# Causal masks written to PSUM by sixteen 32x32 matrix products instead of four 128x128 ones

## Chip, cores and metric

One core of one Trainium2 chip runs the whole program. The time is that of one execution on the device, in microseconds (us). The kernel before takes 2322.14 us (median of 3 executions, 2321.32 to 2324.43).

## The reference

The input is a batch of 32 sequences of 128 tokens with 512 features, and a context of the same shape. Two layers follow, each with an attention part and a feed-forward part. Cut to what matters here:

```python
# x, ctx: (32, 128, 512)
x = x + wkv(w, u, layernorm(x), ctx)            # recurrence over the tokens, per feature

# 16 heads of 32: causal softmax attention
scores = einsum('bhtd,bhsd->bhts', Qf, Kf) * scale
scores = where(tril(ones(T, T)), scores, finfo.min)     # mask
x = x + (softmax(scores) @ V) @ Wp

# mLSTM over q = layernorm(x), k = v = ctx
log_D = where(tril(ones(s, s)), fg_mat, -inf) + ig      # mask
D = exp(log_D - max(log_D)); C = (q @ k) / sqrt(dh) * D
x = x + headnorm((C / normalizer) @ v)

# 32 experts, the best 8 for each token
x = x + moe(layernorm(x), gate_w, w_gate, w_up, w_down)
```

Both masks set every element above (or, transposed, below) the diagonal of a 128 by 128 square to a very low value.

## The kernel before

The program has two blocks. The first does everything up to the router, one sequence of the batch after the other; the second does the experts. The change touches the first block alone.

**The layer loop.** Each engine has its own instruction stream with a function `step(j, ...)`, and the streams meet in semaphores. A pass j of the loop works on four sequences at once: the recurrence of sequence j (flag `ahead`), the softmax attention of j - 1 (`attn`), the mLSTM of j - 2 (`mlstm`), the router of j - 3 (`route`) and the places of the tokens in the experts' lists (`pairs`). Passes 4 to 31 are a hardware loop in which all flags are set, 28 passes; passes 0 to 3 and 32 to 35 are written out with some of the flags off. The order of the calls in `step` is the order of the work on that engine. Nothing else plans it.

**TensorE's pass** (lines 1168 to 1255): turn kn, q product, turn ctx, turn qn (it waits for VectorE's qn), `scores()`, gates, v product, `max_turn()`, `scores_turned()`, `minus_max()`, spread of the gates (L1106) and of the sums (L1102), places (L1165, L1166), turn of yy (it waits for VectorE's yy, L1384), then waits for the places to be taken (L1204) and for ScalarE's copies of the spread gates Lt and Rt (L1207), `log_d()`, qk, row sums, turn of zn, weighted v, centring, head sums, router, heads back (L1145), turn of xn, projection, k product. A "turn" is four 128x128 transposes into one bank of PSUM (L990).

**The masks.** Scores of the 16 heads lie in four banks of PSUM: bank r holds the heads 4c + r, at columns c * 128 for c = 0 to 3. The heads of a bank have their 32 features on partitions 32r to 32r + 31, so the products of the four banks use four different row tiles of the array (32 rows by 128 columns each). Before the products are added, `masks(bank, mask)` writes the mask to each of the four banks: a product of the 128x128 identity (`identb`, bf16) with the mask, which is stored four times side by side (`mask_ts`, `mask_st`, 128 partitions x 4 x 128, bf16), with `start=True`. It is called three times in a pass, in `scores()` with `mask_ts` and in `scores_turned()` and `log_d()` with `mask_st`; the products behind it accumulate onto it.

**The other engines around it.** VectorE in a pass: stats and norm of the next x, the choice of experts, the second residual, qn (L1337), the two scans and the products of the recurrence (L1354 to L1366), the row maximum of the scores (L1400), the gate sums, the ratio (L1378 to yy, L1384), the places (L1510), the first residual x1n (L1389), zn (L1337), four products cm with the exponentials dm (L1449), the best keys, xn, division by the row sums. ScalarE makes the exponentials of the scores (L805) and of log D (L860) and most copies from PSUM, among them Lt (L857) and Rt (L852). GpSimd adds and multiplies for the recurrence, works out the keys (L609 to L625) and issues the indirect DMAs that store the pairs.

**The start.** GpSimd makes the constants (`first_constants`), then waits for VectorE's scales (L667), scales a quarter of the q and k weights (`scale_rows`, L382 to L389) and makes the recurrence's weights gg (L562), for which VectorE's first scan (L1354) waits.

Of the kernel before, what the change touches and what calls it, by code (L numbers as in the profile page):

```python
# [9 lines left out]
ALU = mybir.AluOpType  # L10
# [3 lines left out]
P = 128  # L14
NEG = -1.0e30
# [5 lines left out]
def build(nc, x, ctx_in, w, u, Wa, Wp, w_std, w_rec, Wi, bi, Wf, bf, ln_scale, gate_w, w_gate, w_up,  # L21
          w_down, out, NB=None, NE=None):
    B, T, D = x.shape
# [25 lines left out]
    with ExitStack() as whole:  # L49
# [6 lines left out]
        ps = whole.enter_context(nc.psum_tensor("ps", [P, 8, 512], F32))  # L56
# [29 lines left out]
        with ExitStack() as ctx:  # L86
            def sb(name, shape, dt=F32):
                return ctx.enter_context(nc.sbuf_tensor(name, shape, dt))
# [5 lines left out]
            identb = sb("identb", [P, P], BF16)  # L94
# [3 lines left out]
            mask_ts = sb("mask_ts", [P, 4, P], BF16)  # L98
            mask_st = sb("mask_st", [P, 4, P], BF16)
            zerob = sb("zerob", [P, 4, P], BF16)  # L100
# [370 lines left out]
            def _(pool):  # L471

                def done(a):
                    a.then_inc(pool_step, 1)
                    pool.wait_ge(pool_step, 1)
                    pool.sem_inc(pool_step, -1)
# [23 lines left out]
                def spreads(heads):  # L500
                    for r in heads:
                        q_ = slice(32 * r, 32 * r + 32)
                        put(pick[q_, :, :], 1.0, 0, [[-1, 4], [0, P]])
                        put(bmat[q_, r, 0:DH - 1], 1.0, 0, [[-1, DH - 1]])
                        put(bmat[q_, r, DH:DH + 1], 1.0, 1 - DH, [[0, 1]])
                        done(pool.memset(bmat[q_, r, DH - 1:DH], -1.0))
                        put(bmat[q_, r, DH - 1:DH], 0.0, 1 - DH, [[0, 1]])
                        done(pool.memset(cmat[q_, 32 * r:32 * r + DH - 1], -1.0 / DH))

                def first_constants():  # L510
                    pool.memset(onesb[:, :], 1.0)
                    pool.memset(pick[:, :, :], 0.0)
                    pool.memset(sel_l[:, :], 0.0)
                    pool.memset(sel_r[:, :, :], 0.0)
                    pool.memset(cmat[:, :], 0.0)
                    pool.memset(bmat[:, :, :], 0.0)
                    done(pool.memset(zerob[:, :, :], 0.0))
                    pool.affine_select(out=identb[:, :], in_=zerob[:, 0, :], compare_op=ALU.not_equal, fill=1.0, base=0,
                                       pattern=[[-1, P]], channel_multiplier=1)
                    pool.affine_select(out=ustrict[:, :], in_=zerob[:, 0, :], compare_op=ALU.is_ge, fill=1.0, base=0,  # L520
                                       pattern=[[-1, P]], channel_multiplier=1)
                    pool.affine_select(out=mask_ts[:, :, :], in_=zerob[:, :, :], compare_op=ALU.is_ge, fill=NEG, base=0,
                                       pattern=[[0, 4], [-1, P]], channel_multiplier=1)
                    done(pool.affine_select(out=mask_st[:, :, :], in_=zerob[:, :, :], compare_op=ALU.is_ge, fill=NEG, base=0,
                                            pattern=[[0, 4], [1, P]], channel_multiplier=-1))
                    spreads((0, 1))

                def other_constants():
# [124 lines left out]
                def experts_constants():  # L653
# [9 lines left out]
                    pool.sem_inc(id_ready, 2)  # L663

                first_constants()
                pool.wait_ge(scales_ready, 1)
                pool.sem_inc(scales_ready, -1)  # L667
# [315 lines left out]
            def _(pe):  # L983
# [46 lines left out]
                    m.then_inc(v_ps, 1)  # L1030

                def masks(bank, mask):
                    for r in range(4):
                        pe.matmul(ps[:, bank + r, :], identb[:, :], mask[:, :, :].rearrange("p a t -> p (a t)"),
                                  start=True, stop=False, skip_group_check=True)

                def scores():
                    pe.wait_ge(qk_ready, 1)
                    pe.sem_inc(qk_ready, -1)
                    masks(S_BANK, mask_ts)  # L1040
                    for c in range(4):
                        for r in range(4):
                            m = pe.matmul(ps[:, S_BANK + r, c * T:(c + 1) * T], qs[32 * r:32 * r + 32, c, :],
                                          ks[32 * r:32 * r + 32, c, :], start=False, stop=True, skip_group_check=True)
                    m.then_inc(s_ps, 1)
# [6 lines left out]
                def scores_turned():  # L1052
                    masks(S_BANK, mask_st)
                    for c in range(4):
                        for r in range(4):
                            pe.matmul(ps[:, S_BANK + r, c * T:(c + 1) * T], ks[32 * r:32 * r + 32, c, :],
                                      qs[32 * r:32 * r + 32, c, :], start=False, stop=False, skip_group_check=True)
# [50 lines left out]
                def log_d():  # L1108
                    masks(LD_BANK, mask_st)
                    for r in range(4):  # L1110
                        m = pe.matmul(ps[:, LD_BANK + r, :], Lt[32 * r:32 * r + 32, :],
                                      Rt[32 * r:32 * r + 32, :, :].rearrange("p c t -> p (c t)"),
                                      start=False, stop=True, skip_group_check=True)
                    m.then_inc(l_ps, 1)
# [987 lines left out]
```

## Time and profile before

| | |
|---|---|
| Timed executions | 2322.14 us (2321.32 to 2324.43) |
| Profiled execution, span from the first to the last instruction | 2363.2 us |
| Own time of the profiled execution beyond its span | not given by the page |
| TensorE products busy | 2153.1 us, 91% of the span |
| VectorE busy | 1603.3 us, 68% |
| GpSimd busy | 1489.4 us, 63% |
| ScalarE busy | 1134.5 us, 48% |
| One pass of the layer loop (from one turn of qn to the next) | 35.24 us |
| Layer stage / expert stage | about 0 to 1262 us / 1262 to 2363 us |

A line of a group gives the source line, the engine, the operation, what it writes and reads, the shape and the count; behind the bar stand the busy time in us, the mean duration of one in ns, and the idle time of the engine ahead of it with what ended it. A line in order of time begins with the start and the length in us from the start of the span and covers a run of equal instructions; longer idle time ahead of it stands in brackets, with what ended it. Durations of matrix products include their latency: products in a row start much closer together than they last.

### The profile page before, as it was taken

How to read it: one execution, taken by the hardware profiler on the slowest of the kernel's cores; microseconds unless marked ns; L12 is line 12 of the kernel's file. 1: busy time of each engine (PE TensorE's matmuls, PEld its weight loads, DVE VectorE, ACT ScalarE, POOL GpSimd, SP SyncE). 2: the span in 40 equal slices, each digit the busy share in tenths (PEclk: the TensorE clock that was granted, in tenths of full speed). 3: DMA queues.
4: the chain of work that ended last, by engine and by line, in shares of the span. 5: the costliest groups of instructions: out<-in, count | busy, mean ns of one | idle time of the engine just before them, and what ended most of it. 6: DMA issues, size and time to landing. Idle time of an engine off the chain costs nothing. (4 is left out here: it accounts for less than half of the span.)

```text
span 2363.2 us, 61084 instructions
## 1 busy us (share of the span) xinstructions
PE 2153.1 (91%) x19896; PEld 1618.5 (68%) x19992; DVE 1603.3 (68%) x3221; ACT 1134.5 (48%) x2817; POOL 1489.4 (63%) x1673
## 2 busy tenths in 40 slices
PE   3899999999999999999834999999998999999997
PEld 2677777777767777777523676777776777777775
DVE  5577777777767777777423666666666676666664
ACT  1454554554554554555312544555454555554553
POOL 5226556656656656656456777777776777777775
PEclk9999999999999999999957999999999999999999
DMA  3010010010010010010103888677887788887776
GB/s 121 15 38 27 27 36 27 27 36 27 28 35 27 27 36 27 28 34 23 39 14 92 166 177 186 140 173 169 179 176 177 148 173 182 182 175 154 172 150 98
DMA packets 141437, 222.51 MB, mean 94 GB/s; under 512 B 32944, under 2 KB 65840, under 8 KB 141360
## 3 DMA queue, kind: packets, MB, share of 16 engines
q0 software_dynamic: 74752, 144.02, 31.2%
q1 hardware_dynamic: 62000, 69.24, 9.7%
q10 hardware_dynamic: 4608, 8.39, 0.9%
q8 instruction: 28, 0.46, 0.1%
q14 instruction: 49, 0.40, 0.1%
HBM read 136.34 MB, written 96.73 MB: 99 GB/s over the span
## 5 line engine op out<-in xcount | busy, mean ns | idle before, releaser
L1761 POOL DMA_INDIRECT out_dram<-y,m_add x300 | 501.7, 1672 | 203.6 <-POOLq L1769 143.7
L1887 PE MATMUL ps<-xh,wh 128*128 128x256 f16 x1752 | 399.7, 273 | 7.3 <-PEq L1899 4.7
L1888 PE MATMUL ps<-xh,wl 128*128 128x256 f16 x1752 | 399.5, 273 | 0.0
L1753 POOL DMA_INDIRECT xg<-z_scratch,slot_t x292 | 297.1, 1017 | 94.5 <-issue 86.8
L650 POOL DMA_INDIRECT slot_scratch<-pair,slots x248 | 251.4, 1014 | 99.9 <-issue 41.8
L1964 ACT ACTIVATE y<-ps,wts_now 128x512 f32<-128x512 f32 x294 | 185.5, 682 | 153.8 <-ACTq L1963 149.9
L1016 PEld LDWEIGHTS ps<-xnT,wqk 128*128 128x128 f32 x2048 | 238.7, 194 | 16.9 <-issue 16.9
L1016 PE MATMUL ps<-xnT,wqk 128*128 128x128 f32 x2048 | 241.6, 277 | 1.7 <-PEq L1263 1.7
L1892 PE MATMUL ps<-xl,wh 128*128 128x256 f16 x1752 | 239.0, 273 | 0.0
L2038 DVE SCALAR_TENSOR_TENSOR hx<-ps,s 64x256 f16<-64x256 f32 x146 | 62.2, 426 | 245.6 <-issue 168.6
L1887 PEld LDWEIGHTS ps<-xh,wh 128*128 128x128 f16 x1752 | 171.7, 98 | 53.4 <-issue 21.5
L1888 PEld LDWEIGHTS ps<-xh,wl 128*128 128x128 f16 x1752 | 171.7, 98 | 32.4 <-issue 0.6
L1858 PE MATMUL ps<-ident,xg 128*128 128x128 f32 x1168 | 152.8, 274 | 37.1 <-DMA xg<-z_scratch,slot_t 33.7
L1980 ACT ACTIVATE xh<-ps 128x512 f16<-128x512 f32 x146 | 87.2, 597 | 204.0 <-ACTq L1979 151.0
L1892 PEld LDWEIGHTS ps<-xl,wh 128*128 128x128 f16 x1752 | 171.4, 98 | 19.8
L1858 PEld LDWEIGHTS ps<-ident,xg 128*128 128x128 f32 x1168 | 132.4, 141 | 40.6 <-DMA xg<-z_scratch,slot_t 34.7
L1867 PE MATMUL ps<-dh,hx 128*128 128x512 f16 x294 | 112.2, 382 | 25.2 <-PEq L1864 15.8
L2039 DVE SCALAR_TENSOR_TENSOR h<-ps,s 64x256 f32<-64x256 f32 (+1 forms) x292 | 121.8, 417 | 0.0
L1029 PE MATMUL ps<-wa,xnT 128*128 128x512 f32 x256 | 118.4, 605 | 0.0
L2047 DVE CAST xh<-ps 128x512 f16<-128x512 f32 x146 | 100.1, 685 | 27.0 <-DVEq L2046 18.4
L1875 PE MATMUL ps<-dh,hh 128*128 128x512 f16 x294 | 112.7, 383 | 4.8 <-PEq L1872 3.1
L2055 DVE TENSOR_TENSOR xl<-ps,xh 128x512 f16<-128x512 f32 x146 | 100.9, 691 | 21.5
(279 smaller groups left out, 4659.0 us busy)
## 6 DMA issues: line engine op xcount, KB each, us to landing
wst<-in_L_ffn_w_gate_dram SPq DMA_DIRECT2D x32, 384.0 KB
wst<-in_L_ffn_w_up_dram SPq DMA_DIRECT2D x32, 384.0 KB
xt<-in_x_dram SPq DMA_DIRECT2D x32, 256.0 KB, 2.6
ct<-in_ctx_dram SPq DMA_DIRECT2D x32, 256.0 KB
out_dram<-x SPq DMA_DIRECT2D x32, 256.0 KB
z_scratch<-zn ACTq DMA_DIRECT2D x32, 256.0 KB
wdst<-in_L_ffn_w_down_dram SPq DMA_DIRECT2D x32, 256.0 KB
out_dram<-y,m_add POOLq DMA_INDIRECT x300
```

Of the source, the lines that this page charges most:

```text
L650: pool.indirect_dma_start(out=slot_d[:, :], out_offset=bass.IndirectOffsetOnAxis(ap=slots[:, k:k + 1], axis=0), in_=pair[:, k, :], in_offs ...
L1016: m = pe.matmul(ps[:, bank, c * T:(c + 1) * T], wqk[:, k, j, 4 * c:4 * c + 4, :].rearrange("p h d -> p (h d)"), xnT[:, k, :], start=(k == ...
L1029: m = pe.matmul(ps[:, V_BANK, :], xnT[:, k, :], wa[:, k, 2 * H * DS:2 * H * DS + D], start=(k == 0), stop=(k == KC - 1))
L1753: pool.indirect_dma_start(out=xg[b][:, h, :], out_offset=None, in_=z_d[:, :], in_offset=bass.IndirectOffsetOnAxis(ap=rows(h), axis=0)).the ...
L1761: pool.indirect_dma_start(out=acc_d[:, :], out_offset=bass.IndirectOffsetOnAxis(ap=m_add[:, k, h:h + 1], axis=0), in_=y[:, k, h, :], in_of ...
L1858: m = pe.transpose(ps[:, bank, c0:c0 + P], xg[b][:, h, k * P:(k + 1) * P], ident[:, :])
L1875: pe.matmul(o, hh1[:, t], dh[:, j, 0, :], start=False, stop=False)
L1887: pe.matmul(ps[:, dst, 0:GROUP], wh[:, j, k, c0:c0 + P], xh[:, k, :], start=(k == 0), stop=False)
L1888: pe.matmul(ps[:, dst, 0:GROUP], wl[:, j, k, c0:c0 + P], xh[:, k, :], start=False, stop=False)
L1892: m = pe.matmul(ps[:, dst, 0:GROUP], wh[:, j, k, c0:c0 + P], xl[:, k, :], start=False, stop=(k == KC - 1))
L1964: act.activation(y[:, k, h, :], ps[:, 5 + h, :], ACT.Copy, scale=wts_now[:, h:h + 1])\
L2039: dve.scalar_tensor_tensor(full, up, 1.0 / WSC, s, ALU.mult, ALU.mult).then_inc(dve_step, 1)
```

## The change

`masks` no longer multiplies the whole identity with the mask once for each bank. It issues sixteen products of 32 rows by 32 columns, each with 512 moving columns. The one for column group q (the output partitions 32q to 32q + 31) and bank r uses the row group i = (q + r) mod 4, the block of the identity at row group i, and the mask's copy r on the partitions of row group i. Column group is the outer loop and bank the inner one, so the sixteen use each of the array's sixteen tiles once. The moving operand repeats 128 columns four times by a stride of zero. For this, copy r of the mask is turned by r blocks of 32 rows: its row group i holds the mask's row group (i - r) mod 4. GpSimd builds the copies with 32 selects of 32 partitions x 128, where it used two of 128 partitions x 512, and waits after every eighth (`done`).

```diff
-                    pool.affine_select(out=mask_ts[:, :, :], in_=zerob[:, :, :], compare_op=ALU.is_ge, fill=NEG, base=0,
-                                       pattern=[[0, 4], [-1, P]], channel_multiplier=1)
-                    done(pool.affine_select(out=mask_st[:, :, :], in_=zerob[:, :, :], compare_op=ALU.is_ge, fill=NEG, base=0,
-                                            pattern=[[0, 4], [1, P]], channel_multiplier=-1))
+                    for i in range(4):
+                        for r in range(4):
+                            i_, q_ = slice(32 * i, 32 * i + 32), (i - r) % 4
+                            pool.affine_select(out=mask_ts[i_, r, :], in_=zerob[i_, 0, :], compare_op=ALU.is_ge, fill=NEG,
+                                               base=32 * q_, pattern=[[-1, P]], channel_multiplier=1)
+                            a = pool.affine_select(out=mask_st[i_, r, :], in_=zerob[i_, 0, :], compare_op=ALU.is_ge, fill=NEG,
+                                                   base=-32 * q_, pattern=[[1, P]], channel_multiplier=-1)
+                            if r == 3:
+                                done(a)
...
                 def masks(bank, mask):
-                    for r in range(4):
-                        pe.matmul(ps[:, bank + r, :], identb[:, :], mask[:, :, :].rearrange("p a t -> p (a t)"),
-                                  start=True, stop=False, skip_group_check=True)
+                    for q_ in range(4):
+                        for r in range(4):
+                            i = slice(32 * ((q_ + r) % 4), 32 * ((q_ + r) % 4) + 32)
+                            pe.matmul(ps[32 * q_:32 * q_ + 32, bank + r, :], identb[i, i],
+                                      mask[i, r, :].unsqueeze(1).to_broadcast([32, 4, T]),
+                                      start=True, stop=False, skip_group_check=True)
```

## Rows read from the trace of the kernel before

**Rows 1.** Windows: stretch and length, busy us by engine, clock, DMA share, GB/s.

```profile
200.00:1085.00 885.00, 857.32 (x9414) 643.87 (x9484) 678.32 (x1353) 459.85 (x1152) 516.26 (x775) 1.00 0.10 30
...
1143.00:1152.00 9.00, 6.50 (x51) 4.97 (x53) 2.19 (x1) 1.71 (x3) 2.87 (x3) 0.62 0.02 2
```

**Rows 2.** TensorE's products in order of time, one pass from its turn of qn.

```profile
685.44 0.63 PE L990 MATMUL ps<-ident,qn 128*128 128x128 f32 x4 [2.26 <-PEq L1089]
...
720.64 0.63 PE L990 MATMUL ps<-ident,qn 128*128 128x128 f32 x4
721.36 0.81 PE L1034 MATMUL ps<-mask_ts,identb 128*128 128x512 bf16 x3
722.10 1.17 PE L1043 MATMUL ps<-ks,qs 32*128 32x128 f32 x32
...
728.62 0.27 PE L1050 MATMUL ps<-ident,nm 128*128 128x128 f32 x1
...
732.82 0.18 PE L1166 MATMUL ps<-selacc,onesb 128*128 128x32 bf16 x1
732.85 0.63 PE L990 MATMUL ps<-ident,yy 128*128 128x128 f32 x4
733.93 0.81 PE L1034 MATMUL ps<-mask_st,identb 128*128 128x512 bf16 x3 [0.45 <-PEq L1207]
734.67 1.14 PE L1111 MATMUL ps<-Rt,Lt 32*128 32x512 f32 x8
735.63 1.07 PE L1119 MATMUL ps<-qT,kT 32*128 32x128 f32 x32
```

**Rows 3.** VectorE and ScalarE in order of time, in the same pass.

```profile
719.32 1.17 DVE L1337 TENSOR_SCALAR qn<-x,mv,rstd 128x512 f32<-128x512 f32 x1
...
732.00 0.69 DVE L1384 SCALAR_TENSOR_TENSOR yy<-cv,rden 128x512 f32<-128x512 f32 x1
...
735.84 0.55 DVE L1337 TENSOR_SCALAR zn<-x,mv,rstd 128x512 f32<-128x512 f32 x1
737.19 2.48 DVE L1449 SCALAR_TENSOR_TENSOR cm<-ps,dm 128x512 f32<-128x512 f32 x4 [0.80 <-DVEq L1599]
...
733.47 1.57 ACT L805 ACTIVATE pT<-ps 128x512 f32<-128x512 f32 x3
```

**Rows 4.** Groups by line, TensorE, whole span.

```profile
L1034 PE MATMUL ps<-mask_st,identb 128*128 128x512 bf16 x193 | 52.7, 382 | 17.0 <-PEq L1207 15.2 <-issue 0.2
...
L1068 PE MATMUL ps<-pT,onesf 128*32 128x512 f32 x256 | 34.1, 601 | 1.3 <-PEq L1214 1.1
L1034 PE MATMUL ps<-mask_ts,identb 128*128 128x512 bf16 x96 | 26.5, 386 | 6.2 <-ACT qs L787 2.4 <-PEq L1039 0.8
```

**Rows 5.** TensorE in order of time, windows of 0.1 us or so (PEld: weight load).

```profile
722.10 0.38 PE L1043 MATMUL ps<-ks,qs 32*128 32x128 f32 x2
...
722.10 0.39 PE L1043 MATMUL ps<-ks,qs 32*128 32x128 f32 x4
...
723.20 0.12 PEld L1096 LDWEIGHTS ps<-qT,wg 128*48 128x48 f32 x1
...
736.71 0.64 PE L1068 MATMUL ps<-pT,onesf 128*32 128x512 f32 x4
```

**Rows 6.** GpSimd and VectorE in order of time, at the start.

```profile
6.78 0.29 POOL L520 TENSOR_SCALAR_AFFINE_SELECT ustrict<-zerob 128x128 bf16<-128x128 bf16 x1
7.03 0.64 POOL L522 TENSOR_SCALAR_AFFINE_SELECT mask_ts<-zerob 128x512 bf16<-128x512 bf16 x1
...
8.48 0.63 POOL L479 TENSOR_SCALAR_AFFINE_SELECT pick<-pick 32x512 f32<-32x512 f32 x1 [0.22 <-POOLq L476]
...
17.08 0.83 POOL L382 TENSOR_TENSOR wqk<-wa,scl 128x384 f32<-128x384 f32 x1 [3.63 <-POOLq L667]
...
24.14 1.30 POOL L562 TENSOR_TENSOR gg<-gam,ex 128x512 f32<-128x512 f32 x1
...
27.36 1.22 DVE L1354 TENSOR_TENSOR_SCAN sq_<-dtab,gg 128x512 f32<-128x512 f32 x1 [0.26 <-DVEq L1353]
```

## The prediction, made before the changed kernel was run

> **What bounds the kernel now.** I read the page first (TensorE is its busiest engine), then the windows by stage, one pass of the layer loop in order of time on TensorE and on the other engines, the groups of the mask line, and last the start. Between 200 and 1085 us, where the masks are laid, TensorE is busy 857 of 885 us at the full granted clock, 2.4 GHz [rows 1]. That looks like a stage in which every saved TensorE nanosecond counts. It is not quite so.
>
> In the pass from 720.64 us on, TensorE turns qn at 720.64, and VectorE finished qn at 719.32 + 1.17 = 720.49; it turns yy at 732.85, and VectorE finished yy at 732.00 + 0.69 = 732.69 [rows 2, 3]. Both times TensorE starts 0.15 us behind the data, about the price of a handover: it has no idle time to show there, yet the data comes no earlier. From qn to yy VectorE works 12.2 us on its own recurrence (it takes the row maximum of the scores only after its scans), so a TensorE that is quicker between 720.64 and 732.82 waits for yy instead. Two of the three mask groups lie exactly there (721.36, and behind the turn of nm at 728.62). The third (733.93) lies behind the turn of yy, and it waits 0.45 us for ScalarE's copy of Rt [rows 2]. Behind it the chain is products, exponentials (ScalarE), VectorE's cm at 737.19 with 0.80 us of idle before it [rows 3], turn of zn, the rest of the pass, the next qn. What the third group gains is gained by the pass.
>
> **The mask group, before and after.** Before: four 128x512 products, 0.215 us apart ((0.81 - 0.38)/2), one record of the four missing, and the next line's products start 0.31 us behind the last one's start: 0.215 of streaming and 0.09 of emptying, because the shape of the tile changes [rows 2]. First product 0.215 before the first record, so 733.72 to 734.67 is 0.95 us a group, 96 groups (289 of 384 records) [rows 2, 4].
>
> After: sixteen 32x32 products of 512 columns on sixteen different tiles. No row shows this shape. Bounds from the nearest: two row tiles fill 0.38 us and four 0.39, so they start some 0.007 apart, and four column tiles of 512 columns, 0.60 us each, lie inside 0.64 [rows 4, 5]. At that pace: load of the first tile 0.03, fifteen starts 0.10, one stream 0.215, emptying 0.09, together 0.44 us. The other end: the sixteen go by fours, 0.03 + 4 x 0.215 + 0.09 = 0.98. I take 0.44, since both kinds of tile overlap in the trace and the new group only crosses them.
>
> The new shape costs one more emptying, ahead of the group. A lone product of 128 columns is 0.27 us (728.62), so the last product of the 32x128 line starts at 722.10 + 1.17 - 0.27 = 723.00, and the next shape's load is at 723.20: 0.20 for its streaming and the emptying [rows 2, 5]. So a turn whose last product starts at T lets tiles start at T + 0.20. Groups 1 and 2: from the last turn product (720.64 + 0.63 - 0.27 = 721.00) to the products it was 1.10 us (722.10), and becomes 0.20 + 0.44 = 0.64: 0.46 less each.
>
> **What of it reaches the end of a pass.** The first two groups put 0.9 us into the wait for yy; through the turn of yy none of it passes. They do make Rt 0.9 us earlier, so the 0.45 us wait in front of group 3 goes, and what is late next is the turn itself: last product 732.85 + 0.63 - 0.27 = 733.21, tiles at 733.41, products at 733.41 + 0.44 = 733.85 instead of 734.67. That is **0.82 us**. Is something late behind it? The qk line (735.63 before) would start at 734.81 and needs the attention exponentials, which end at 733.47 + 1.57 = 735.04 but move 0.9 earlier with the scores, to 734.1, and VectorE's x1n: turn of yy done at 733.48, a handover of 0.15 and 0.69, 734.3. VectorE's zn ends at 736.39 and cm starts at 737.19: it can follow by 0.80 to 0.88 us (VectorE's neighbours overlap by 0.08), so the cap and the gain are the same size [rows 2, 3]. Everything later is released by cm or by TensorE behind it and moves along, GpSimd's key work included, which also starts earlier because the places are known earlier. Per pass 0.82, between 0 (groups by fours, below) and 0.88.
>
> 28 passes of the loop: 28 x 0.82 = 23.0. The five passes around it lay masks too: the first has no third group and a late row maximum (0.4), the second and third about 0.6 and 0.8; the last with scores runs two groups partly at half clock, where a group costs double (a granted clock of 0.62 is left between 1143 and 1152) [rows 1], and has no turn of yy (1.9), and one more third group at half clock (0.8): 4.5 together, an estimate from the same two group prices.
>
> **The start.** GpSimd built two masks in 0.64 us each, 1.23 together; now it builds 32 pieces of 32 x 128. By the 128x128 select at 6.78, 0.25 ahead of the next, that is 8.0, and three more handshakes of 0.22 idle (8.48) and the overlap lost with each make 8.8: 7.6 us more [rows 6]. It had finished its constants at 13.5 us (the row at 17.08 has 3.63 idle) and would finish at 21.1, so scaling and gg (ends 25.44) come 4.15 later, 29.6; VectorE was ready for gg at 27.1 and started its scan at 27.36 [rows 6]. So the start costs 29.6 + 0.1 - 27.36 = **2.3 us**; everything behind the scan moves along. If a select of 32 partitions costs only 0.1, the cover of 3.4 us hides it all: 0. At 0.29 each with no overlap it is 3.8.
>
> **Sum.** 2.3 - 23.0 - 4.5 = -25.2 us. The page gives only the span of the profiled execution, 2363.2 us, and no time for what lies around it; it is 41 us above the median of the timed runs, 2322.14. The terms are differences inside the layer stage, where hardly any DMA runs (10% share [rows 1]), so I carry them over unscaled: 2322.1 - 25.2 = **2297 us** (span 2338).
>
> **Rivals.**
> - A, each product holds the array's entrance for some 28 ns, whatever its tile. The 32-column product at 732.82 and the turn at 732.85 start 0.03 apart, although 32 columns stream in 0.013 by the 0.215 of 512; and row tiles, 0.007 apart in a four, average 0.028 over a line ((1.17 - 0.27)/32) [rows 2, 5]. Then a group is 0.03 + 15 x 0.028 + 0.215 + 0.09 = 0.755, the pass gains 734.67 - (733.41 + 0.755) = 0.505: 28 x 0.505 = 14.1, + 3 at the ends, - 2.3: 15 less, 2307. Against it: the starts 0.007 apart are of products with loads of their own. The Trainium skill (TensorE: Matmul & The Clock Gate, Part 1) says that start-to-start never drops below some 25 ns however small the product; by that rule the time would be 2306, and the trace agrees for products on one tile but not for four different tiles.
> - B, slower: the chip lets only one row tile at a time write a bank. The order is column group outside, bank inside, and bank r is written from a different row tile in each round, so round 2 waits for round 1: four waves, 0.98 a group. In the trace every row tile has its own bank, so nothing excludes it; column tiles share a bank freely [rows 5]. Groups 1 and 2 then cost 0.20 + 0.98 = 1.18 instead of 1.10 and 1.05 (0.08 and 0.13 more), Rt and all behind it are 0.2 later: 28 x 0.2 + 2.3 = 8 more, 2330. It decides as soon as a group costs more than about 0.9. The Trainium skill (TensorEngine Tiling (Array Packing), Gotcha 1: PSUM Pressure) states that different row tiles cannot access the same PSUM bank simultaneously; whether that costs time or is no matter for different partitions of a bank, no row shows.
> - C, the clock falls: TensorE now idles about 0.8 us before the turn of yy in each pass. Half clock on even 5 us of a pass would cost 2.5 us, 70 in all, 2370. Against it: 2.26 us idle before 685.44 lies in a stretch with the granted clock at full [rows 1, 2]; the clock of 0.62 stands behind the loop.
> - D, part of the 0.82 is caught by VectorE or GpSimd (their accesses to one memory port slow each other: qn took 1.17 us and zn, the same operation, 0.55 [rows 3]). Half lost: 28 x 0.4 + 3 - 2.3 = 12 less, 2310.
>
> **Chances.** Forecast 0.60, A 0.20, D 0.09, B 0.07, C or all sixteen in series (hundreds of us) 0.04. A measurement of this kernel can tell about 0.2%, 4.6 us. Faster by more: forecast, A and most of D, 0.87; within: the rest of D and some of B, 0.05; slower: 0.08. The range goes from 2290 (gain 0.88, start free, ends 5) to 2315 (half of A's gain); B and C stay outside.
>
> **What would show it.** Right: mask products 0.007 to 0.01 apart, 0.44 from the first to the next line; a wait of TensorE for yy (some 0.8 us) where there was none; no wait for Rt; cm with hardly any idle before it; a pass of 34.4 us instead of 35.24; the scan of gg at 29.7. Starts some 0.028 apart show A, fours 0.215 apart B, a pass of 35.4 with B's waves. Wrong would be a pass shorter than 34.3 (then VectorE's chain was not what set it), or one unchanged though the group is 0.44.

## The result: half of the forecast gain, and the profile after

Over four runs of each on one chip the changed kernel takes 2311.56 us (2308.04 to 2314.27) and the kernel before 2323.28 us (2321.32 to 2329.36): a ratio of 0.9942, 95% interval 0.9930 to 0.9953. The gain is small (0.6%) but clear of the interval. The time lies inside the range of 2290 to 2315; the gain is 11.7 us where the sum had 25.2.

The profiled execution of the changed kernel has a span of 2309.7 us (2311.45 with what lies around it). The windows first, as in [rows 1]; the second and third ones are one pass, and a stretch in a later one:

```profile
200.00:1085.00 885.00, 850.00 (x10547) 641.81 (x10540) 684.05 (x1374) 466.90 (x1167) 512.85 (x787) 0.98 0.10 30
...
822.60:857.00 34.40, 33.04 (x416) 25.07 (x414) 27.04 (x55) 18.36 (x47) 20.41 (x32) 1.00 0.09 31
...
870.10:873.60 3.50, 3.50 (x44) 2.18 (x40) 1.79 (x5) 2.15 (x5) 1.63 (x7) 0.51 0.30 75
```

The pass is 34.40 us, as forecast. But the granted clock of the loop, 1.00 before, is 0.98, and 870.10 shows why: 3.5 us at half clock, 1.2 GHz. TensorE in order of time, the undisturbed pass (it answers to [rows 2]):

```profile
822.12 0.63 PE L995 MATMUL ps<-ident,qn 128*128 128x128 f32 x4
822.68 0.43 PE L1041 MATMUL ps<-mask_ts,identb 32*32 32x512 bf16 x16
823.04 1.17 PE L1051 MATMUL ps<-ks,qs 32*128 32x128 f32 x32
824.15 1.07 PE L1104 MATMUL ps<-qT,wg 128*48 128x128 f32 x8
825.06 1.04 PE L1104 MATMUL ps<-kT,wg 128*48 128x128 f32 x8
...
833.26 0.18 PE L1174 MATMUL ps<-selacc,onesb 128*128 128x32 bf16 x1
834.32 0.63 PE L995 MATMUL ps<-ident,yy 128*128 128x128 f32 x4 [0.88 <-PEq L1010]
834.87 0.43 PE L1041 MATMUL ps<-mask_st,identb 32*32 32x512 bf16 x16
835.24 1.14 PE L1119 MATMUL ps<-Rt,Lt 32*128 32x512 f32 x8
836.20 1.07 PE L1127 MATMUL ps<-qT,kT 32*128 32x128 f32 x32
...
838.82 0.63 PE L995 MATMUL ps<-ident,zn 128*128 128x128 f32 x4 [0.48 <-PEq L1159]
```

A group, from its first product to the next line's, is now 0.36 or 0.37 us (822.68 to 823.04, 834.87 to 835.24). The wait for Rt is gone, and a wait of 0.88 us for yy stands where TensorE had none. Its starts within a group, from three narrow windows (to 822.70, 822.72 and 822.73), which answer to [rows 5]:

```profile
822.68 0.40 PE L1041 MATMUL ps<-mask_ts,identb 32*32 32x512 bf16 x7
...
822.68 0.42 PE L1041 MATMUL ps<-mask_ts,identb 32*32 32x512 bf16 x13
...
822.68 0.43 PE L1041 MATMUL ps<-mask_ts,identb 32*32 32x512 bf16 x16
```

All sixteen start within 0.05 us, some 3.3 ns apart. The groups by line, for [rows 4], where the turns of yy had no wait worth a row:

```profile
L995 PE MATMUL ps<-ident,yy 128*128 128x128 f32 x128 | 21.5, 294 | 46.3 <-PEq L1010 46.3
L1041 PE MATMUL ps<-mask_st,identb 32*32 32x512 bf16 x1024 | 29.2, 402 | 1.4 <-PEq L1215 1.4
L1041 PE MATMUL ps<-mask_ts,identb 32*32 32x512 bf16 x512 | 13.9, 385 | 0.4 <-PEq L1047 0.4
```

VectorE in the same pass (for [rows 3]), with cm right behind zn, and GpSimd and VectorE at the start (for [rows 6]):

```profile
833.48 0.69 DVE L1392 SCALAR_TENSOR_TENSOR yy<-cv,rden 128x512 f32<-128x512 f32 x1
...
837.30 0.62 DVE L1345 TENSOR_SCALAR zn<-x,mv,rstd 128x512 f32<-128x512 f32 x1
837.85 2.47 DVE L1457 SCALAR_TENSOR_TENSOR cm<-ps,dm 128x512 f32<-128x512 f32 x4
```

```profile
7.01 0.28 POOL L525 TENSOR_SCALAR_AFFINE_SELECT mask_ts<-zerob 32x128 bf16<-32x128 bf16 x1
...
15.50 0.29 POOL L527 TENSOR_SCALAR_AFFINE_SELECT mask_st<-zerob 32x128 bf16<-32x128 bf16 x1
...
27.86 1.26 POOL L567 TENSOR_TENSOR gg<-gam,ex 128x512 f32<-128x512 f32 x1
...
29.27 1.23 DVE L1362 TENSOR_TENSOR_SCAN sq_<-dtab,gg 128x512 f32<-128x512 f32 x1 [4.75 <-DVEq L1361]
```

And a pass that went wrong, whose log D products run into the half clock of 870.10:

```profile
868.71 0.63 PE L995 MATMUL ps<-ident,yy 128*128 128x128 f32 x4 [0.88 <-PEq L1010]
869.27 0.44 PE L1041 MATMUL ps<-mask_st,identb 32*32 32x512 bf16 x16
869.64 1.68 PE L1119 MATMUL ps<-Rt,Lt 32*128 32x512 f32 x8
871.08 1.95 PE L1127 MATMUL ps<-qT,kT 32*128 32x128 f32 x32
```

1.68 and 1.95 us instead of 1.14 and 1.07. Nine of the 28 passes are so: the clock falls 12.3 to 13.7 us behind the turn of qn, at or soon behind the turn of yy (12.2), and they last 35.4 to 35.9 us, 1.25 more on average, 11.2 in all. The kernel before has no such pass. The mean granted clock is 0.968 in the profiled execution and 0.966 to 0.970 in the three others, so nothing sets this one apart.

### The profile page after: what moved, and what is told of

Its sections match the earlier page's. It is cut to its first block and busy times, and to the rows that moved or that the text cites. A ratio compares the mean times of both kernels' runs of the same rounds, so it can differ in the third digit from the quotient of the medians.

```text
span 2309.7 us, 63546 instructions
## 1 busy us (share of the span) xinstructions
PE 2121.0 (92%) x21143; PEld 1611.5 (70%) x21144; DVE 1597.4 (69%) x3221; ACT 1137.5 (49%) x2817; POOL 1486.4 (64%) x1703
## 5 line engine op out<-in xcount | busy, mean ns | idle before, releaser
L1988 ACT ACTIVATE xh<-ps 128x512 f16<-128x512 f32 x146 | 87.2, 597 | 219.0 <-ACTq L1987 219.0
L1092 PE MATMUL ps<-wp,oT 128*128 128x512 f32 x256 | 115.2, 593 | 0.0
```

The source lines that it names most:

```text
L1092: m = pe.matmul(ps[:, PR_BANK, :], oT[:, k, :], wp[:, k, :], start=(k == 0), stop=(k == KC - 1))
```

## The experiments

Twelve runs on three chips, each with its own runs of the kernel before: e1, e2, e3 and e5 on the first, e4, e6, e7 and e8 on the second, e9 to e12 on the third. These are other chips than that of the result, and the kernel before takes 2358 to 2366 us there, so that only ratios and the layer stage (from the span's start to the expert stage's first gather into xg) are compared. "Pass" is the median. "Scores" is the time from the first score product to the first gate product of kT (823.04 to 825.06 above). Passes with a fall are counted among the 26 inner ones: the 28 of the hardware loop without the two around the one long wait of every run, for x in the 16th pass (2.2 us, the 2.26 in [rows 2]).

| kernel | ratio (95%) | pass | scores | idle before yy | passes with a fall | layer stage |
|---|---|---|---|---|---|---|
| before | 1 | 35.24 | 2.01 | none | 0 | 1262.5 |
| changed | 0.9942 (0.9930 to 0.9953) | 34.40 | 2.01 | 0.88 | 9 | 1241.9 |
| e1_before_again | 1.0003 (0.9991 to 1.0014) | 35.24 | 2.01 | none | 0 | 1259.0 |
| e2_fill_yy | 0.9978 (0.9967 to 0.9989) | 34.87 | 2.97 | filled | 0 | 1251.8 |
| e3_third_only | 0.9981 (0.9969 to 0.9992) | 34.93 | 2.01 | none | 0 | 1253.0 |
| e5_second_third | 0.9918 (0.9906 to 0.9931) | 34.43 | 2.01 | 0.34 | 0 | 1237.3 |
| e6_after_again | 0.9960 (0.9947 to 0.9973) | 34.86 | 2.98 | 0.13 | 0 | 1251.4 |
| e4_half_whole | 0.9954 (0.9941 to 0.9967) | 34.83 | 2.01 | 0.70 | 0 | 1251.1 |
| e7_start_split | 0.9980 (0.9970 to 0.9990) | 34.86 | 2.98 | 0.13 | 0 | 1253.5 |
| e8_second_third_split | 0.9923 (0.9910 to 0.9936) | 34.43 | 2.01 | 0.34 | 0 | 1242.3 |
| e9_late_copies | 0.9910 (0.9893 to 0.9926) | 34.43 | 2.01 | 0.34 | 0 | 1244.9 |
| e10_quarter_whole | 1.0018 (1.0005 to 1.0030) | 34.83 | 2.26 | 0.87 | 8 | 1264.8 |
| e11_narrow_whole | 1.0064 (1.0047 to 1.0081) | 35.71 | 2.95 | none | 0 | 1275.6 |
| e12_after_third | 0.9964 (0.9950 to 0.9978) | 34.90 | 3.02 | 0.20 | 0 | 1256.4 |

The theory (I, idle): the changed kernel lets TensorE idle for 0.88 us ahead of yy in a pass that idles elsewhere too, and in some passes the clock falls behind it. Its rival (S, shape): the new tiles bring the clock down.

**e1_before_again**: the kernel before, unchanged.

> The kernel before, unchanged, profiled once more. The changed kernel's layer stage ended 20.6 us earlier in its profile (first gather of the experts at 1241.9 us instead of 1262.5), the timed medians differ by only 11.7. Theory: the layer stage of the kernel before repeats (passes of 35.24 us, first gather at 1262 +- 2 us), and what differs between its profile and its timed executions is the expert stage, 1100.7 us in the profile, here nearer 1060; time 2322 +- 3. Rival: the layer stage itself varies, passes or the first gather differ from 1262.5 by 5 us or more.

The passes are 35.24 us, as expected. The rest is not: the first gather comes at 1259.0 us, 3.5 earlier, so the layer stage of one kernel varies by more than the 2 us expected; the expert stage takes 1092.7 us and not some 1060; and the time is 2358.9 us, on a slower chip. Its trace has all four records of a group, and so shows that the wait for Rt is 0.235 us and not the 0.45 of [rows 2]: there the first record of the group was missing, and its 0.215 us counted as idle.

**e2_fill_yy**: the changed kernel, with something to do in the gap.

```
  (behind the wait for VectorE's copy of s1, ahead of the turn of yy)
+ for _ in range(3):
+     pe.matmul(ps[:, YT_BANK, :], identb[:, :], zerob as 512 columns, start=True, stop=True)
```

> The changed kernel with three 128x128 products of 512 columns of zeros added into the bank of the yy turn, just ahead of that turn, in the passes that wait there (0.65 us in a wait of 0.88). Theory I (the idle time ahead of the yy turn lets the clock fall): no pass at half clock any more, all at 34.40 us, 11 us less than the changed kernel, about 2300. Theory S (the 32x32 products themselves count too little as work): the falls stay in about nine of 28 passes, time unchanged at 2311. Theory N (falls come from the start or from chance): passes at half clock at other places, between the two.

No clock falls in the inner passes, with all 48 tile products in every pass: the tiles alone don't bring the clock down. But the pass is 34.87 instead of 34.40: the scores take 0.96 us longer, so TensorE comes that much later to the gap, and the turn of yy lies 12.76 us behind that of qn instead of 12.20. TensorE stalled there in all 26 inner passes, and nothing that was changed explained it. So this run doesn't test the filler: the stall alone closes the gap to 0.13 us (e6 below, the same kernel without filler), and no clock falls there either.

**e3_third_only** and **e5_second_third**: fewer groups of tiles.

```
+ def whole_masks(bank, mask):
+     for r in range(4):
+         pe.matmul(ps[:, bank + r, :], identb[:, :], mask[:, 0, :].unsqueeze(1).to_broadcast([P, 4, T]), ...)
- masks(S_BANK, mask_ts)          group 1: e3 and e5
+ whole_masks(S_BANK, mask_ts)
- masks(S_BANK, mask_st)          group 2: e3 alone
+ whole_masks(S_BANK, mask_st)
```

> Groups 1 and 2 laid by four 128x128 products again (from the unturned copy of the mask), only the third group, of log D, by sixteen tiles. TensorE arrives at the yy turn as before (idle under 0.05 us), Rt comes as late as before. The tiles start at 733.69 in the numbering of the pass before and take 0.37, so the products start at 734.05 instead of 734.67: a pass of 34.62 us, 28 x 0.62 = 17 and 3 at the ends, 2 for the start: 18 less than before, 2305, with no falls of the clock under theory I. Theory S: some falls stay, 2309 to 2315. If instead TensorE's whole busy time set the pass, a third of 3 x 0.59 or so would go, 0.5 of it with all three groups in proportion.

> Group 1 by four 128x128 products again, groups 2 and 3 by tiles. Group 2 alone makes Rt 0.5 us earlier, which is all that the third group's wait of 0.45 us can use: pass of 34.40 us as with all three, TensorE idle ahead of yy only 0.4 us instead of 0.88. Theory I: falls of the clock gone or rare, 2300 to 2303. Theory S: falls in some six passes, 2307 to 2311.

e5 is the fastest layer stage of all and settles what the change could have given: passes of 34.43 with the idle time at 0.34 us and no fall. TensorE and VectorE in one of them:

```profile
547.00 0.63 PE L995 MATMUL ps<-ident,yy 128*128 128x128 f32 x4 [0.35 <-PEq L1010]
547.55 0.44 PE L1041 MATMUL ps<-mask_st,identb 32*32 32x512 bf16 x16
...
549.99 0.55 DVE L1350 TENSOR_SCALAR zn<-x,mv,rstd 128x512 f32<-128x512 f32 x1
550.54 2.48 DVE L1462 SCALAR_TENSOR_TENSOR cm<-ps,dm 128x512 f32<-128x512 f32 x4
```

The first group of tiles gains nothing (34.40 against 34.43). e3 misses by 0.3 us a pass: the wait for Rt stays, and the qk products wait 0.11 us more, so that cm starts only 0.31 us earlier than before. The second group is what makes Rt and the exponentials early.

**e6_after_again** and **e4_half_whole**: the changed kernel once more, and an idle gap without tiles. e4 leaves out the masks of two heads in four in groups 1 and 2.

```
- masks(S_BANK, mask_ts)          (and mask_st)
+ half_masks(S_BANK, mask_ts)     ps[:, bank + r, 0:2 * T] <- identb, mask[:, 0:2, :]
```

> The changed kernel once more, beside the two kernels that follow. Theory I (TensorE idles 0.9 us ahead of every turn of yy, and in some passes the granted clock falls behind it): the first qn turn some 3.6 us later than in the kernel before; passes of 34.4 us, but again 6 to 12 of the 28 with a stretch of half clock and 35.4 to 35.9 long; the layer stage 20 us shorter (18 to 23), the ratio 0.994. Theory S (the 32x32 tiles themselves bring the clock down) says the same of this kernel. If the nine slow passes were a whim of one execution, none or some twenty are slow here, and the layer stage is 31 or 8 us shorter.

> The kernel before, with the four whole-identity products of groups 1 and 2 cut to 256 of 512 columns (the other half of the heads stays unmasked in these two); group 3 untouched, and no 32x32 tile anywhere. Two groups are 0.43 us shorter each, so TensorE idles some 0.9 us ahead of the turn of yy as in the changed kernel; group 3 stays at 0.95 us, and through the turn of yy only the 0.235 us wait for Rt goes: passes of 35.0 us at full clock, 28 x 0.235 = 6.6 us. Theory I: the granted clock falls behind the wait for yy in 6 to 12 passes here too, 7 to 15 us lost again, so the layer stage is 0 to 8 us longer than with no fall: ratio 0.998 to 1.003. Theory S: no clock falls within the loop, ratio 0.996 to 0.997.

Both missed. The same kernel as in the result has passes of 34.86 us here, no fall in the 26 inner passes (two in the passes ahead of the hardware loop, where the stall is absent and the idle time ahead of yy is 1.36 and 0.97 us), and e2's stall:

```profile
716.78 0.63 PE L995 MATMUL ps<-ident,qn 128*128 128x128 f32 x4
717.34 0.43 PE L1041 MATMUL ps<-mask_ts,identb 32*32 32x512 bf16 x16
717.70 1.21 PE L1051 MATMUL ps<-ks,qs 32*128 32x128 f32 x23
719.28 0.56 PE L1051 MATMUL ps<-ks,qs 32*128 32x128 f32 x9 [0.37 <-issue]
719.77 1.07 PE L1104 MATMUL ps<-qT,wg 128*48 128x128 f32 x8
...
728.89 0.18 PE L1174 MATMUL ps<-selacc,onesb 128*128 128x32 bf16 x1
729.19 0.63 PE L995 MATMUL ps<-ident,yy 128*128 128x128 f32 x4
```

"issue" is time in which TensorE waits for nothing that the profile shows. The 23rd product and its neighbours trickle, the line takes 2.07 us instead of 1.11, and all behind it is 0.96 us late; the gates' chain on ScalarE (5.06 us behind the turn of qn instead of 4.09) makes VectorE's yy 0.2 later, and the late exponentials make the qk products wait. So the pass loses 0.46 us, about what the falls cost in the result (11.2 / 28 = 0.40). e4 has 0.70 us of idle time in the inner passes and no fall: either theory would live with that, and it bounds I from below. It gained 0.41 a pass where 0.235 was expected. The idle figure begins at the end of the last turn product, whose latency it leaves out; by starts, the wait for Rt cost more: the third group begins 13.08 us behind the turn of qn in e1 and 12.66 in e4, 0.42 apart.

**e7_start_split** and **e8_second_third_split**: the changed kernel, and e5, with half of the selects later.

```
- pool.affine_select(out=mask_st[i_, r, :], ...)        in first_constants
- step(0, attn=False, mlstm=False, route=False, pairs=False, late=False)
+ weigh_cc()
+ weigh_gg()
+ (the sixteen selects of mask_st, done(a) after every fourth)
+ add_past_weights()
+ hold_ctx()
```

> The changed kernel, with the sixteen selects of mask_st moved in GpSimd's order from the constants to behind gg of the first step (16 x 0.245 = 3.9 us). First turn of yy 1.9 us earlier than in the changed kernel (36.3 us instead of 38.2), since its scaling and gg come before VectorE's scan again. If the half clock at 64 and 71 us comes from the late start, the first qn turn is 3.6 us earlier (84.1); if it comes from the idle ahead of yy in pass 1, 1.9 us (85.8). The loop as in the changed kernel. Ratio 0.0008 to 0.0015 below the changed kernel's, 0.9925 to 0.9932.

> Group 1 by four whole products, groups 2 and 3 by tiles (as in e5_second_third), and the sixteen selects of mask_st moved behind gg of the first step. Theory I: TensorE's idle ahead of yy is 0.4 us, no clock falls in the loop, every pass 34.4 us, and the start is 1.9 to 3.6 us shorter than in e5_second_third, so ratio 0.990 to 0.991 against the kernel before, 0.003 to 0.004 below the changed kernel: the best of all. If the start is hidden elsewhere by now, it ties with e5_second_third at 0.992.

Missed: the first turn of yy comes at 39.9 us, 1.7 later than in the changed kernel. gg's scan starts at 27.33 as it should, but GpSimd's addition into cc, which VectorE's denominator needs, now stands behind the selects:

```profile
26.05 1.17 POOL L713 TENSOR_SCALAR_AFFINE_SELECT mask_st<-zerob 32x128 bf16<-32x128 bf16 x4
27.45 3.75 POOL L713 TENSOR_SCALAR_AFFINE_SELECT mask_st<-zerob 32x128 bf16<-32x128 bf16 x4 [0.22 <-POOLq L476]
31.41 1.42 POOL L713 TENSOR_SCALAR_AFFINE_SELECT mask_st<-zerob 32x128 bf16<-32x128 bf16 x4 [0.22 <-POOLq L476]
33.06 1.04 POOL L713 TENSOR_SCALAR_AFFINE_SELECT mask_st<-zerob 32x128 bf16<-32x128 bf16 x4 [0.22 <-POOLq L476]
34.47 1.26 POOL L579 TENSOR_TENSOR cc<-cc,sq_ 128x508 f32<-128x508 f32 x1 [0.38 <-POOLq L578]
```

and the four selects that run at the same time as VectorE's scan and products take 3.75 us instead of 1.04. e8's loop repeats e5's, and e8 beats the changed kernel on the same chip (e6): the two intervals don't meet. Its start is no shorter than e5's (first turn of qn at 87.2 and 85.5 us).

**e9_late_copies**: e5, with one unturned mask_ts, and mask_st's pieces in other_constants.

```
+ done(pool.affine_select(out=mask_ts[:, 0, :], in_=zerob[:, 0, :], ...))      first_constants
+ (the sixteen selects of mask_st, done(a) after every fourth)                 other_constants
```

> Group 1 by four whole products, groups 2 and 3 by tiles, as in e5_second_third; of mask_ts one unturned copy is built (a 128x128 select), and the sixteen pieces of mask_st are built in other_constants, behind GpSimd's cc addition and its copy of vT, where GpSimd idles 4.46 us before 55.11 and TensorE asks for the constants only at some 52 us. GpSimd's first constants are then one select shorter than in the kernel before: first turn of yy at 36.3 us or 0.2 earlier (38.3 in e5_second_third), first qn turn at 82.5 to 84.9 (85.5), passes of 34.43 us with no fall of the clock in them, layer stage 24 us shorter than before; ratio 0.990, 0.001 below e5_second_third and 0.005 below the changed kernel. If the idle of GpSimd is not where it seems, the gain over e5_second_third is nothing (0.992).

Half right. The first turn of yy comes at 35.8 us, the earliest of all. But the 4.46 us of GpSimd's idle before 55.11 were no slack: GpSimd had asked for the zeroing of the scratch and waited for it to land (4.88 us now), so that its next cc comes 3.3 later and the first turn of qn 5.7 later (91.2 against 85.5); between the two, e9 has 10.2 us at half clock (from 64.0 and 74.2), and e5 none. The two ratios, on two chips, can't be told apart.

**e10_quarter_whole**: as e4, on 128 of 512 columns, three heads in four unmasked in groups 1 and 2.

> The kernel before, with the products of groups 1 and 2 cut to 128 of 512 columns (three heads of four stay unmasked there); no 32x32 tile, group 3 untouched. Each group 0.65 us shorter, so TensorE idles 1.1 us ahead of the turn of yy (0.70 in e4_half_whole, 0.88 in the changed kernel). Theory I (the length of that idle stretch brings the half clock, at some point between 0.70 and 0.88 us): the granted clock falls behind the wait in a third or more of the passes, which last 35.8 to 36.3 instead of 34.8: layer stage 7 us or more longer than in e4_half_whole, ratio 0.998 to 1.001. If the stretch doesn't matter (the falls of the changed kernel belong to the tiles, or to that one execution), passes of 34.8 and ratio 0.995 as in e4_half_whole.

What theory I says of it comes: with the whole-identity products alone and an idle time of 0.87 us, eight of the 26 inner passes are slow, 36.3 to 36.5 us instead of 34.83 (and one more ahead of the loop, with 1.20 us idle). One of them, and the window behind its wait:

```profile
517.49 0.63 PE L990 MATMUL ps<-ident,yy 128*128 128x128 f32 x4 [0.89 <-PEq L1005]
518.31 1.48 PE L1034 MATMUL ps<-mask_st,identb 128*128 128x512 bf16 x3 [0.19 <-issue]
519.72 1.97 PE L1116 MATMUL ps<-Rt,Lt 32*128 32x512 f32 x8
```

```profile
518.00:521.40 3.40, 3.21 (x13) 1.22 (x15) 2.18 (x4) 0.64 (x2) 2.05 (x8) 0.50 0.21 68
```

A quarter of the mask work was left in two groups of three, and the kernel is slower than with all of it.

The length of this one gap isn't isolated, though. Where it is longer, TensorE is also idle for longer in the pass as a whole (waits over 0.1 us add up to 1.35 us in the changed kernel, 1.30 in e10, 1.11 in e4, 0.95 in e6, 0.71 in e5), and no run has the one without the other. What speaks for the gap is where the clock falls: 12.3 to 13.7 us behind the turn of qn in the changed kernel, 12.7 to 13.2 in e10, with the turn of yy at 12.2 in both. Nor is 0.70 a safe length elsewhere: in pass 2, ahead of the loop, the clock fell behind 0.77 us in e5 and 0.78 in e9, and didn't behind 0.77 in e8.

**e11_narrow_whole**: the kernel before, with group 1 in as many instructions as the tiles are. It masks one head in four there.

```
- masks(S_BANK, mask_ts)
+ for q_ in range(4):
+     for r in range(4):
+         pe.matmul(ps[:, bank + r, 32 * q_:32 * q_ + 32], identb[:, :], mask[:, 0, 32 * q_:32 * q_ + 32], ...)
```

> The kernel before, with group 1 as sixteen whole-identity products of 32 columns (one head of four masked there): as many instructions as the sixteen tiles, and at about 0.028 us each (0.45) as short, but no 32x32 tile. It tells apart two theories of the 0.97 us by which TensorE stalls within the 32 score products of e6_after_again, e7_start_split and e2_fill_yy, always near the 203rd load or product behind the loop's jump back. Theory F (instructions are supplied too slowly when so many short ones stand close behind the jump): the same stall, 0.3 to 1.0 us in the score products of every pass, and TensorE idles 0 to 0.3 us ahead of yy. Theory T (it belongs to the 32x32 tiles): no stall, score products in 1.1 us, and 0.4 to 0.5 us of idle ahead of yy. Ratio 0.996 to 1.000 by either.

Theory T is refuted, and the stall is the one that F expects; the ratio is above the range expected. The same stall without a tile:

```profile
510.10 0.63 PE L990 MATMUL ps<-ident,qn 128*128 128x128 f32 x4
510.61 0.55 PE L1040 MATMUL ps<-mask_ts,identb 128*128 128x32 bf16 x16
511.09 1.18 PE L1049 MATMUL ps<-ks,qs 32*128 32x128 f32 x23
512.64 0.56 PE L1049 MATMUL ps<-ks,qs 32*128 32x128 f32 x9 [0.37 <-issue]
```

In all five runs with sixteen products in group 1 on these chips it begins at about the 203rd load or product in order of time behind the record of the loop's jump back, which lies 6.4 us ahead of the turn of qn (some 33 of them belong to the product ahead of the jump, still under way), and it ends 2.5 us behind the turn. With four products in group 1 the 203rd comes later and doesn't stall (e1, e3, e5); e10, the quickest with four, stalls by 0.25, in the gate products. In the pass with the long wait (e6), where the jump lies 8.7 us ahead of the turn, the place is some sixteen records further on, and the end still 2.5 us behind the turn; so neither a fixed count nor a fixed time from the jump fits all passes. That TensorE lacks instructions there is inferred from this: no row shows how they are supplied. e11 pays for the stall in full, since TensorE had nothing to spare ahead of yy: kT's gate products start 3.95 instead of 3.48 us behind the turn of qn, and the pass is 0.47 longer.

**e12_after_third**: the changed kernel, third time, on e9 to e11's chip.

> The changed kernel once more, on the chip of the three above. In one execution it ran with passes of 34.40 us and nine falls of the clock, in another (e6_after_again) with 34.86 and the stall in the score products and no fall. By both theories it shows one of these two pictures here, ratio 0.994 to 0.996; a picture between them (stall in some passes, falls in the others) would say that both come and go from pass to pass.

The picture of e6 again, on another chip. So two of the three profiled executions of the changed kernel stall, and the one that doesn't has the falls. Why TensorE doesn't stall there is open.

## Why the prediction was right or wrong

**What bounds the pass, right.** The chain qn, VectorE, yy, products, cm set the pass: the first group of tiles gained nothing (e5 against the result), and all of TensorE's gain ahead of yy became a wait (0.88; some 0.8 was forecast). 34.4 us was forecast and 34.40 measured. The close agreement owes something to the cap: behind the turn of yy the products of the third group came 0.91 us earlier in the pass (13.12 us behind the turn of qn instead of 14.03), not 0.82, and VectorE's zn let cm come only 0.83 earlier (15.73 instead of 16.56), about the cap that the prediction had named. With cm right behind zn, a still quicker third group would gain nothing.

**The group, right in kind, sized wrong.** 0.44 was forecast, 0.365 measured: the starts are 3.3 ns apart and not 7 (0.05 less), and the 0.03 for the load of the first tile doesn't stand between the first product and the next line's. With 0.215 of streaming, 0.10 is left for the emptying, where 0.09 was taken. Rival A (28 ns an instruction) and B (four waves in a bank) are both refuted by 822.68 to 822.73. The rule that the Trainium skill gives (TensorE: Matmul & The Clock Gate, Part 1), no start within some 25 ns of the last, holds in these traces for products on one tile (e11's sixteen narrow ones start 25 ns apart) and not from tile to tile. Gotcha 1 of its page TensorEngine Tiling (Array Packing) costs no time here: four row tiles write four quarters of one bank, with starts some 13 ns apart and streams of some 0.2 us, and the group of 0.365 us leaves no room for waves.

**The wait for Rt, missized, without harm.** As idle time it was 0.235 us and not 0.45 (e1), by starts 0.42 (e4). The 0.82 didn't rest on it, since what counted was the turn of yy behind it.

**The 23.0 of the loop: this failed, by rival C.** 28 passes at 0.84 would be 23.5. In the profiled execution nine of them lost 11.2 to the clock, so 12.3 were left. C was named, its place was right, and it was put aside by one row: 2.26 us idle at full clock before 685.44. That one idle stretch was no evidence for one that comes back every 34 us; and the clock does fall within 1.6 us of that very turn, the one with 2.2 us of idle time ahead of it, in ten of the twelve experiments (not in e1 and e6). Its price was off as well: a third of the passes and 1.25 us each, not every pass and 2.5. Where the clock held (e6, e12), theory F's stall took 0.46 us a pass, 28 x 0.46 = 12.9, which no rival had: the sum counted each instruction's time on the array and nothing else.

**That the time fell inside the range was luck.** The upper part of the range, to 2315, was made for half of A's gain, and C was said to stay outside. A was refuted; C came, at a third of the passes, and took 11.2 us of the 25.2. On two other chips the same kernel gained 0.4% (e6, e12), with no falls in the inner passes but with the stall, which no rival had.

**The start, 2.3 forecast, 1.9 measured at the scan** (29.27 against 27.36) and at the first turn of yy (38.2 against 36.3). The selects were 0.245 apart each as assumed. At the first turn of qn it is 3.6 us (87.7 against 84.1), with the clock at half from 64.6 and 71.4, 3.4 us each; e6, with one such stretch, has 2.1 over the same row, e12, with two, 3.8.

**The ends, 4.5 forecast, not to be seen.** From the 30th turn of qn to the first gather the two executions of the kernel before take 154.3 and 149.9 us, the three of the changed one 143.5, 151.2 and 153.1: the half clock comes and goes there, by more than the term.

**The sum.** 3.6 - (29 x 0.85 - 11.2) = -9.9 at the 30th turn of qn, by the two profiled executions, and the medians say -11.7. What is left is within the ends' own scatter. The expert stage (1100.7 us in the profile of before, 1067.8 after; 1092.7 in e1) differs between executions of one kernel, and the change doesn't touch it. Two figures of the prediction don't fit its own rows, and nothing rested on them: the lower bound of 0 us a pass for groups by fours, where rival B has 0.2 longer, and the range's lower end of 2290, which by its own terms (28 x 0.88 and 5) is 2292.5.

## What to carry to other kernels

Time saved on an engine that then waits isn't free: in two kernels with a wait of 0.87 or 0.88 us in every pass TensorE went to half clock in a third of them, so speed up only the groups behind which the data are late. Here two groups of three beat all three, chip by chip: 0.9923 against 0.9960 (e8, e6) and 0.9910 against 0.9964 (e9, e12). On those two chips it was the stall that they avoided. Count instructions as well as time: sixteen short ones for four, close behind a loop's jump, cost TensorE 0.94 to 1.00 us on three chips of four. One quiet row where the clock held is no evidence that it will.

## What the runs showed of the hardware

- Products on sixteen different 32x32 tiles start 3.3 ns apart (822.68 to 822.73), four quarters of one bank are written at once, and sixteen take 0.365 us with the emptying, against 0.95 for four products of the whole array. Narrow products on the whole array start 25 ns apart (e11).
- Passes with 0.88 or 0.87 us of idle time ahead of yy had stretches of 3.4 us at 1.2 GHz in 9 and 8 of the 26 inner ones, with tiles (the changed kernel) and without (e10); with 0.70 (e4), 0.34 (e5, e8, e9) and less there were none. How much of it is the gap and how much the idle time of the whole pass is not separated.
- Some 200 loads and products behind the record of a loop's jump back TensorE stood still until 2.5 us behind the turn of qn, whatever the products were (e2, e6, e7, e11, e12). The Trainium skill (Runtime: NRT & Kernel Launch, Instruction fetch mechanics) says that a sequencer fills its instruction memory by blocks of 256 instructions and that a taken branch to a block that isn't there stalls it until the fetch. The stall here comes not at the jump but behind it, so that no run shows this rule; why it comes there, and why one chip shows nothing, is open.
